# GAT layer and soft mixture of experts on one core: TensorE multiplies a step's share of the attention products before, not after, it turns the step's weights

## The chip, the core and the metric

The kernel runs on one core of one Trainium2 chip. A core has five engines with instruction streams of their own: TensorE (PE; its weight loads are listed as PEld), VectorE (DVE), ScalarE (ACT), GpSimd (POOL) and SyncE (SP), which here issues the transfers. They meet only through semaphores. The metric is the device time of one execution in microseconds (us). Before the change the median of three runs is 1707.67 us (1706.31 to 1708.2).

## The reference

1250 nodes with 768 features pass a two-layer graph attention network over 41250 edges (random edges both ways, and a loop at each node), and then a soft mixture of four experts; each adds to its input. The change lies in the first attention layer, with eight heads of 128 channels:

```
h = (x @ W1.T).reshape(n, 8, 128)
a_src = einsum('nhc,hc->nh', h, att_src);  a_dst = einsum('nhc,hc->nh', h, att_dst)
e = leaky_relu(a_src[src] + a_dst[dst], 0.2)
alpha = exp(e - segment_max(e, dst)[dst]);  alpha = alpha / segment_sum(alpha, dst)[dst]
out = segment_sum(alpha[:, :, None] * h[src], dst) + bias;  h1 = relu(out)
```

The second layer has one head of 768 channels. Everything is float32 at the interface.

## The kernel before

Edges are not followed one by one. The first stage builds a dense matrix `ln_c` with the logarithm of how often each source meets each destination (a large negative number where there is no edge), 1250 by 1250, in ten tiles of 128 destinations. With it, attention is dense: `attend_heads` (L911 to L1158) computes, for each head and each tile of destinations, a 128 by 1250 piece of logits, its softmax numerators, and their product with the head's features.

A **step** k is one head and one tile of destinations: head k // 10, tile j = k % 10, 80 steps in all. What each engine does for a step:

- POOL adds the row of the sources' part to the counts: `base` (L1006), two buffers deep.
- ACT computes relu of the scaled sum into PSUM, `at_r` (L1016), one buffer; it issues relu(k + 1) ahead of exp(k).
- DVE adds the two and takes the row maximum in one instruction, `logits(k)` (L1068), into a ring `q` of three; then negates the maximum (L1071).
- ACT takes the exponent of `q` in place (L1040), and reads the row sum off; that releases `at_p`.
- PE **turns** the step's weights: ten 128x128 transposes of `q` by the identity into `at_t` (L1134), three banks of PSUM, of which there is one set. Each bank is written once the step before has been read out of it.
- The turned weights are copied to `pt`: two banks by DVE (`read_turned(k - 1)`, L1077, after `logits(k)`), the third by ACT (L1044, after `exp(k)`). These copies release `at_read_low`, `at_read_mid` and `at_read_top`.
- PE multiplies: a head's output is made in three **chunks** of 4, 3 and 3 destination tiles, `DST_CHUNKS = ((0, 4), (4, 3), (7, 3))`. A chunk takes ten float32 products `at_o += h * pt` (L1155), one per tile of sources. They are dealt out to the steps by the table `PRODUCTS`; each entry is a chunk, how many heads back, the first source tile and how many:

```
    ((1, 1, 7, 3),), ((2, 1, 0, 3),), ((2, 1, 3, 4),), ((2, 1, 7, 3),),
    ((0, 0, 0, 3),), ((0, 0, 3, 2),), ((0, 0, 5, 3),), ((0, 0, 8, 2),), ((1, 0, 0, 3),), ((1, 0, 3, 4),),
```

So chunk 0 of a head is multiplied at j = 4 to 7, chunk 1 at j = 8, 9 and 0 of the next head, chunk 2 at j = 1, 2 and 3 of the next head. Ahead of a chunk's first product PE waits for two things: that all copies of the chunk's own destination tiles are made (for chunk 0 the last of them is step j = 3), and that the output bank, one of two, is free, which `at_h1_lo` tells.

A finished chunk is divided by the row sums, gets its bias and relu (DVE L1095 and L1097, three steps after its last product), is rounded to f16 by ACT (L1029), and the rest is stored by DVE (`low`, L1103), one step later; `low` releases `at_h1_lo`. Chunk 0 ends at j = 7, so its `low` is issued on DVE at j = 1, behind `read_turned` of the step before. The inverse row sums go through DRAM and back by transfers on SP (L982, L988), one chunk after the other. After step 79 no weights are left to turn; PE finishes the last products, and for the last chunk spreads the inverse sums itself (L1142). Every engine leaves the block before the second layer starts.

All orders here are written out by hand in the loops; no scheduler moves anything.

Of the kernel before, what the change touches and what calls it, by code (L numbers as in the profile page):

```python
# [32 lines left out]
P = 128  # L33
N = 1250
NT = -(-N // P)
# [17 lines left out]
BANK = 512  # L53
# [857 lines left out]
def attend_heads(nc, mem, sem, const, ln_c, h, h1, nad, s_row, in_s, bias_col, in_bias, a_rows, inv_rows):  # L911
# [8 lines left out]
    STEPS = HEADS * NT  # L920
    RING = 3
    base = mem("base", [P, 2, NP], F32)
    q = mem("q", [P, RING, NP], F32)
# [10 lines left out]
    neg_ready, p_ready, p_turned = sem("at_neg"), sem("at_p"), sem("at_pt")  # L934
    read_low, read_mid, read_top = sem("at_read_low"), sem("at_read_mid"), sem("at_read_top")
# [7 lines left out]
    def chunk_tiles(g):  # L943
        head, c = divmod(g, CHUNK)
        return head, DST_CHUNKS[c][0], DST_CHUNKS[c][1]


    def slices(k):
        head, j = divmod(k, NT)
        for c, back, first, units in PRODUCTS[j]:  # L950
            if 0 <= head - back < HEADS:
                yield (head - back) * CHUNK + c, first, units
# [9 lines left out]
    with (  # L962
# [6 lines left out]
        @block.sync  # L969
        def _(eng):  # L970
            def load_s(head):
                eng.wait_ge(in_s, 16 * head)
                eng.wait_ge(relu_ready, (head - 1) * NT)
                eng.wait_ge(base_ready, (head - 1) * NT)
                eng.dma_start(s_row[:, head % 2, :].rearrange("p (t n) -> p t n", t=NT),
                              a_rows[head * NT:(head + 1) * NT, :].unsqueeze(0).to_broadcast([P, NT, P]))\
                    .then_inc(in_s, 16)

            def turn_inverse(g):
                head, a, n = chunk_tiles(g)  # L980
                eng.wait_ge(factor_ready, g + 1)
                eng.dma_start(inv_rows[g, 0:n * P].rearrange("(t p) -> p t", p=P),  # L982
                              factor[:, head * NT + a:head * NT + a + n],
                              allow_slow_non_contiguous=True).then_inc(inv_kept, 16)
                eng.wait_ge(inv_kept, 16 * (g + 1))
                if g >= 2:
                    eng.wait_ge(divided, g - 1)
                eng.dma_start(inv[:, g % 2, 0:n * P],  # L988
                              inv_rows[g:g + 1, 0:n * P].to_broadcast([P, n * P])).then_inc(in_inv, 16)

            for head in range(HEADS):
                for c in range(CHUNK):
                    if head * CHUNK + c < LAST:
                        turn_inverse(head * CHUNK + c)
                    if c == CHUNK - 1 and head + 2 < HEADS:
                        load_s(head + 2)
# [128 lines left out]
        @block.tensor  # L1125
        def _(eng):
            for k in range(STEPS + NT):
                if k < STEPS:
                    eng.wait_ge(p_ready, k + 1)
                    for b, read in enumerate((read_low, read_mid, read_top)):  # L1130
                        if k >= 1:
                            eng.wait_ge(read, k)
                        for t in range(b * (BANK // P), min((b + 1) * (BANK // P), NT)):
                            mm = eng.transpose(tp[:, t * P:(t + 1) * P], q[:, k % RING, t * P:(t + 1) * P],  # L1134
                                               const["ident"][:, :])
                        mm.then_inc(p_turned, 1)
                if k == STEPS + 1:
                    n = chunk_tiles(LAST)[2]
                    eng.wait_ge(read_low, STEPS)
                    eng.wait_ge(spread_ready, n)  # L1140
                    for i in range(n):
                        mm = eng.matmul(tp[:, i * P:(i + 1) * P], const["ones"][:, :], spread[:, i * P:(i + 1) * P],  # L1142
                                        start=True, stop=True)
                    mm.then_inc(inv_turned, 1)
                for g, first, units in slices(k):
                    head, a, n = chunk_tiles(g)
                    if first == 0:

                        last = head * NT + a + n
                        for read in (read_low, read_mid, read_top):  # L1150
                            eng.wait_ge(read, last)
                        if g >= 2:
                            eng.wait_ge(h1_lo, g - 1)
                    for t in range(first, first + units):
                        mm = eng.matmul(op[:, g % 2, 0:n * P], h[:, head, t, :], pt[:, a:a + n, t, :],  # L1155
                                        start=t == 0, stop=t == NT - 1, skip_group_check=True)
                    if first + units == NT:
                        mm.then_inc(out_done, 1)  # L1158


def second_layer(nc, mem, sem, banks, const, ln_c, pn, pt, h1t, z, v2, x2t, xw, w2t, fw1, bias, x_in, a_rows, x_out, phi,
# [1084 lines left out]
```

## Time and profile before

| | |
|---|---|
| median of 3 runs | 1707.67 us |
| the profiled execution | 1710.9 us, its span 1709.1 us |
| steps of the first attention layer | from 316.9 us (first turn) to 619.6 us (last `low`) |
| in that stretch (316.9 to 620): PE, DVE, ACT, POOL busy | 278.2, 264.8, 244.6, 218.9 us of 303.1 |
| idle PE ahead of the turns, waiting for ACT's exponent | 35.9 us, 33 times, of which 16.5 before the first |
| granted TensorE clock in that stretch, mean | 0.96 |

The span is what the profiler saw of one execution; the profiled execution's own time is 1.8 us longer. Busy times overlap, because the engines work side by side. A clock of 1.00 is 2.4 GHz, 0.50 is 1.2 GHz. In rows of the timeline the columns are the start in us, how long the row's instructions took together, the engine, line and operation, output<-inputs, shapes and xcount; brackets at the end give the idle time before the row and what ended it. Instructions in a row are merged where they follow each other. The profiler lists two records for each float32 product of L1155 and one for each transpose, so x6 is three products, x8 four and x4 two.

### The profile page before, as it was taken

The page shows a single profiled execution, that of the slowest core. Times are in us where ns is not written, and L with a number is a line of the kernel's source. Part 1 is how long each engine was busy: PE and PEld are TensorE (multiplying, and loading weights), DVE is VectorE, ACT ScalarE, POOL GpSimd, SP SyncE. Part 2 cuts the span into 40 slices and gives each one's busy share as a digit, 9 for nine tenths or more (in the row PEclk, how much of TensorE's full clock was granted, in tenths as well). Part 3 has the DMA queues.
Part 4 walks back from the last instruction along what each step waited for, and adds up shares of the span by engine and source line. Part 5 has one row for each costly group of instructions (what it writes and reads, how often), then busy time and mean ns, then how long its engine had stood idle before and what let it go on. Part 6 is the DMA issues. An engine that isn't in the chain of part 4 may idle for free. (4 is left out here: it accounts for less than half of the span.)

```text
span 1709.1 us, 24928 instructions
## 1 busy us (share of the span) xinstructions
PE 1557.3 (91%) x8615; PEld 882.5 (52%) x8615; DVE 1102.0 (64%) x1810; ACT 846.2 (50%) x1322; POOL 272.4 (16%) x120
## 2 busy tenths in 40 slices
PE   6896666599999989999999899999999989999999
PEld 3442332366666545555554455555555545555555
DVE  7989999699999937553332456666666666766200
ACT  3159999688888827421111333333333335656000
POOL 1000000687877707000000000000000000000000
PEclk9998889699999989999999999999999998999999
DMA  4000100023232336441210544444444446783211
GB/s 180 19 29 27 44 19 11 4 34 37 32 50 34 22 81 164 103 134 56 56 47 28 133 116 117 116 117 117 119 119 119 119 124 206 214 214 98 74 56 53
DMA packets 204683, 146.91 MB, mean 86 GB/s; under 512 B 171758, under 2 KB 173768, under 8 KB 204464
## 3 DMA queue, kind: packets, MB, share of 16 engines
q1 hardware_dynamic: 204592, 145.75, 33.8%
q8 instruction: 51, 0.84, 0.3%
q14 instruction: 40, 0.33, 0.1%
HBM read 78.70 MB, written 28.35 MB: 63 GB/s over the span
## 5 line engine op out<-in xcount | busy, mean ns | idle before, releaser
L1006 POOL TENSOR_TENSOR base<-s_row,ln_c 128x1250 f32<-128x1250 f32 x80 | 227.6, 2847 | 58.5 <-DVE top L1068 56.2
L102 PE MATMUL sl_di<-x2t_hi,ph_hi 128*128 128x512 f16 (+1 forms) x576 | 195.5, 339 | 0.3 <-PEq L1226 0.3
L104 PE MATMUL sl_di<-x2t_hi,ph_lo 128*128 128x512 f16 (+1 forms) x576 | 195.5, 339 | 0.0
L103 PE MATMUL sl_di<-x2t_lo,ph_hi 128*128 128x512 f16 (+1 forms) x576 | 195.5, 339 | 0.0
L1155 PE MATMUL at_o<-pt,h 128*128 128x384 f32 (+1 forms) x480 | 188.2, 530 | 1.9 <-DVE h L1103 1.9
L901 PE MATMUL fs<-one_src,one_dst 128*128 128x512 f16 x720 | 120.4, 324 | 63.7 <-ACT one_dst L812 54.6
L1134 PE MATMUL at_t<-ident,q 128*128 128x128 f32 x800 | 108.1, 285 | 36.7 <-ACT q L1040 35.9
L1134 PEld LDWEIGHTS at_t<-ident,q 128*128 128x128 f32 x800 | 93.6, 146 | 79.7 <-ACT q L1040 69.7
L647 DVE TENSOR_SCALAR one_src<-iota,src,worth 128x625 f16<-128x625 f16 x360 | 131.9, 442 | 3.2 <-PE fs L901 2.1
L1016 ACT ACTIVATE at_r<-s_row,nad 128x1250 f32<-128x1250 f32 x80 | 104.5, 1307 | 37.8 <-DVE top L1068 37.1
L901 PEld LDWEIGHTS fs<-one_src,one_dst 128*128 128x128 f16 x720 | 56.8, 106 | 126.9 <-ACT one_dst L812 73.2
L1068 DVE CUSTOM_DVE_ANT_0 q<-at_r,base 128x1250 f32<-128x1250 f32 x80 | 116.2, 1453 | 5.5 <-POOL base L1006 3.6
L1077 DVE COPY pt<-at_t 128x512 f32<-128x512 f32 x160 | 103.2, 685 | 23.0 <-PE at_t L1134 22.6
L1155 PEld LDWEIGHTS at_o<-pt,h 128*128 128x128 f32 x480 | 86.8, 194 | 57.5 <-issue 27.6
L2076 PE MATMUL co_c<-hid_hi,ps_hi 128*128 128x385 f16 x320 | 105.9, 331 | 8.7 <-DVE ps_lo L2010 8.7
L102 PE MATMUL sl_di<-xw,pt_hi 128*128 (+1 forms) x320 | 105.3, 329 | 7.4 <-DMA pt_lo<-pn_lo 5.7
L1787 DVE TENSOR_REDUCE top<-lg 128x1 f32<-128x1250 f32 x32 | 46.5, 1454 | 98.4 <-ACT lg L1721 86.0
L1040 ACT ACTIVATE q<-q,neg_top 128x1250 f32<-128x1250 f32 x80 | 105.9, 1323 | 0.1
L2080 PE MATMUL co_c<-hid_hi,ps_lo 128*128 128x385 f16 x320 | 105.4, 329 | 0.0
L103 PE MATMUL sl_di<-xw,pt_hi 128*128 (+1 forms) x320 | 105.3, 329 | 0.0
L104 PE MATMUL sl_di<-xw,pt_lo 128*128 (+1 forms) x320 | 105.3, 329 | 0.0
L2078 PE MATMUL co_c<-hid_lo,ps_hi 128*128 128x384 f16 x320 | 105.0, 328 | 0.0
(270 smaller groups left out, 3137.9 us busy)
## 6 DMA issues: line engine op xcount, KB each, us to landing
logits_t<-lg SPq DMA_DIRECT2D x32, 625.0 KB, 3.2
phf<-in_phi SPq DMA_DIRECT2D x32, 384.0 KB, 3.5
logits_in<-logits_t SPq DMA_DIRECT2D x16, 640.0 KB, 5.5
logits_in<-logits_t SPq DMA_DIRECT2D x16, 610.0 KB, 5.3
w2f<-in_w2t SPq DMA_DIRECT2D x16, 384.0 KB, 3.4
s_row<-a_rows SPq DMA_DIRECT2D x9, 640.0 KB, 6.5
ew1f<-in_fw SPq DMA_DIRECT2D x6, 768.0 KB, 5.3
wf<-in_fw SPq DMA_DIRECT2D x12, 384.0 KB, 6.2
```

The costliest lines, as they stand in the source:

```text
L102: eng.matmul(out, lh, rh, start=first, stop=False, skip_group_check=True)
L103: eng.matmul(out, lh, rl, start=False, stop=False, skip_group_check=True)
L104: return eng.matmul(out, ll, rh, start=False, stop=last, skip_group_check=True)
L647: eng.tensor_scalar(one_src[:, place(b, i), 0:HALF], const["iota"][:, 0:HALF], src[:, ds(col, 1)], worth[:, ds(col, 1)], ALU.is_equal, ALU ...
L901: mm = eng.matmul(counts(g)[:, a:a + n], one_dst[:, place(b, i), :], one_src[:, place(b, i), a:a + n], start=False, stop=b == PIECES - 1 a ...
L1006: eng.tensor_tensor(base[:, k % 2, 0:N], s_row[:, head % 2, 0:N], ln_c[:, j, 0:N], ALU.add)\
L1040: eng.activation(q[:, k % RING, 0:N], q[:, k % RING, 0:N], ACT.Exp, bias=neg_top[:, k:k + 1], accum_out=den[:, k:k + 1]).then_inc(p_ready, 1)
L1068: eng.tensor_tensor_reduce(q[:, k % RING, 0:N], rp[:, 0:N], base[:, k % 2, 0:N], 1.0, -MASK / 2, ALU.add, ALU.max, top[:, k:k + 1]).then_i ...
L1134: mm = eng.transpose(tp[:, t * P:(t + 1) * P], q[:, k % RING, t * P:(t + 1) * P], const["ident"][:, :])
L1155: mm = eng.matmul(op[:, g % 2, 0:n * P], h[:, head, t, :], pt[:, a:a + n, t, :], start=t == 0, stop=t == NT - 1, skip_group_check=True)
L2076: eng.matmul(cp[:, bank, 0:HID + 1], high, hid[0][:, slot, 0:HID + 1], start=begin, stop=False, skip_group_check=True)
L2080: mm = eng.matmul(cp[:, bank, 0:HID + 1], low, hid[0][:, slot, 0:HID + 1], start=False, stop=end, skip_group_check=True)
```

## The change

In PE's loop over the steps the block that turns the step's weights moves from the head of the loop body to its end, behind the products dealt to that step. Waits, counts and tiles stay as they are; so do the programs of the other engines.

```
             for k in range(STEPS + NT):
-                if k < STEPS:
-                    eng.wait_ge(p_ready, k + 1)
-                    for b, read in enumerate((read_low, read_mid, read_top)):
-                        if k >= 1:
-                            eng.wait_ge(read, k)
-                        for t in range(b * (BANK // P), min((b + 1) * (BANK // P), NT)):
-                            mm = eng.transpose(tp[:, t * P:(t + 1) * P], q[:, k % RING, t * P:(t + 1) * P],
-                                               const["ident"][:, :])
-                        mm.then_inc(p_turned, 1)
                 if k == STEPS + 1:
...
                 for g, first, units in slices(k):
...
                     if first + units == NT:
                         mm.then_inc(out_done, 1)
+                if k < STEPS:
+                    eng.wait_ge(p_ready, k + 1)
+                    for b, read in enumerate((read_low, read_mid, read_top)):
...
+                        mm.then_inc(p_turned, 1)
```

PE's program around the first product of a chunk 0 (step j = 4 of the second head), before. `at_t` rows are transposes, `at_o` rows products, of 512 columns for chunk 0 and 384 for the others:

```order
L1155 MATMUL at_o<-pt_10595,h_95 128x384 x3
L1134 MATMUL at_t<-ident_49,q_10594 128x128 [waits at_read_low,at_p]
L1134 MATMUL at_t<-ident_49,q_10594 128x128 x3
L1134 MATMUL at_t<-ident_49,q_10594 128x128 [waits at_read_mid]
L1134 MATMUL at_t<-ident_49,q_10594 128x128 x3
L1134 MATMUL at_t<-ident_49,q_10594 128x128 [waits at_read_top]
L1134 MATMUL at_t<-ident_49,q_10594 128x128
L1155 MATMUL at_o<-pt_10595,h_95 128x512 [waits at_read_top,at_h1_lo,at_read_mid,at_read_low]
L1155 MATMUL at_o<-pt_10595,h_95 128x512 x2
```

Here the ten transposes are those of step j = 4, the products ahead of them those of j = 3. The same place now:

```order
L1146 MATMUL at_o<-pt_10595,h_95 128x384 x3
L1156 MATMUL at_t<-ident_49,q_10594 128x128 [waits at_read_low,at_p]
L1156 MATMUL at_t<-ident_49,q_10594 128x128 x3
L1156 MATMUL at_t<-ident_49,q_10594 128x128 [waits at_read_mid]
L1156 MATMUL at_t<-ident_49,q_10594 128x128 x3
L1156 MATMUL at_t<-ident_49,q_10594 128x128 [waits at_read_top]
L1156 MATMUL at_t<-ident_49,q_10594 128x128
L1146 MATMUL at_o<-pt_10595,h_95 128x512 [waits at_read_top,at_h1_lo,at_read_mid,at_read_low]
L1146 MATMUL at_o<-pt_10595,h_95 128x512 x2
L1156 MATMUL at_t<-ident_49,q_10594 128x128 [waits at_read_low,at_p]
```

The rows read alike, but the transposes ahead of the chunk's first product are now those of step j = 3, whose copies that product waits for; those of j = 4 stand behind it, in the last row. The step's products have moved ahead by one set of transposes.

PE's program from j = 0 to j = 1 of the second head, where chunk 2 of the first head starts, before (the first row is j = 0, the transposes are those of j = 1):

```order
L1155 MATMUL at_o<-pt_10595,h_95 128x384 x3
L1134 MATMUL at_t<-ident_49,q_10594 128x128 [waits at_read_low,at_p]
L1134 MATMUL at_t<-ident_49,q_10594 128x128 x3
L1134 MATMUL at_t<-ident_49,q_10594 128x128 [waits at_read_mid]
L1134 MATMUL at_t<-ident_49,q_10594 128x128 x3
L1134 MATMUL at_t<-ident_49,q_10594 128x128 [waits at_read_top]
L1134 MATMUL at_t<-ident_49,q_10594 128x128
L1155 MATMUL at_o<-pt_10595,h_95 128x384 [waits at_read_top,at_h1_lo,at_read_mid,at_read_low]
```

And now:

```order
L1146 MATMUL at_o<-pt_10595,h_95 128x384 x3
L1156 MATMUL at_t<-ident_49,q_10594 128x128 [waits at_read_low,at_p]
L1156 MATMUL at_t<-ident_49,q_10594 128x128 x3
L1156 MATMUL at_t<-ident_49,q_10594 128x128 [waits at_read_mid]
L1156 MATMUL at_t<-ident_49,q_10594 128x128 x3
L1156 MATMUL at_t<-ident_49,q_10594 128x128 [waits at_read_top]
L1156 MATMUL at_t<-ident_49,q_10594 128x128
L1146 MATMUL at_o<-pt_10595,h_95 128x384 [waits at_read_top,at_h1_lo,at_read_mid,at_read_low]
L1146 MATMUL at_o<-pt_10595,h_95 128x384 x2
L1156 MATMUL at_t<-ident_49,q_10594 128x128 [waits at_read_low,at_p]
```

Again the transposes between are a step earlier: those of j = 0 now, with those of j = 1 behind the product. DVE's `low` of j = 1, on which `at_h1_lo` counts, stands on DVE behind the copies of j = 0.

## Rows read from the trace of the kernel before

**Rows 1.** Windows of the attention steps: three heads' worth, then all of it.
```profile
core 0: us, PE busy (x) PEld busy (x) DVE busy (x) ACT busy (x) POOL busy (x), PEclk, DMA share, GB/s
402.00:438.00 36.00, 33.99 (x163) 21.69 (x162) 33.69 (x64) 31.46 (x48) 28.94 (x11) 1.00 0.31 38
...
316.90:620.00 303.10, 278.17 (x1286) 178.87 (x1286) 264.79 (x493) 244.56 (x365) 218.91 (x77) 0.96 0.27 31
```

**Rows 2.** Waits between 317 and 602 us: waiter, waited for, us in total, times, longest.
```profile
PE at_t L1134 <- ACT q L1040: 35.9, 33, 16.5
```

**Rows 3.** Timeline of PE, one head and the next's start (j = 4 to j = 4).
```profile
439.44 1.31 PE L1134 MATMUL at_t<-ident,q 128*128 128x128 f32 x10 [0.37 <-ACT q L1040]
440.58 2.74 PE L1155 MATMUL at_o<-pt,h 128*128 128x512 f32 x6
443.16 1.26 PE L1134 MATMUL at_t<-ident,q 128*128 128x128 f32 x10
444.25 1.88 PE L1155 MATMUL at_o<-pt,h 128*128 128x512 f32 x4
445.97 1.26 PE L1134 MATMUL at_t<-ident,q 128*128 128x128 f32 x10
...
450.39 1.31 PE L1134 MATMUL at_t<-ident,q 128*128 128x128 f32 x10 [0.59 <-ACT q L1040]
...
454.83 2.10 PE L1155 MATMUL at_o<-pt,h 128*128 128x384 f32 x6
456.77 1.25 PE L1134 MATMUL at_t<-ident,q 128*128 128x128 f32 x10
457.86 2.75 PE L1155 MATMUL at_o<-pt,h 128*128 128x384 f32 x8
460.44 1.25 PE L1134 MATMUL at_t<-ident,q 128*128 128x128 f32 x10
461.53 2.10 PE L1155 MATMUL at_o<-pt,h 128*128 128x384 f32 x6
...
471.42 1.26 PE L1134 MATMUL at_t<-ident,q 128*128 128x128 f32 x10
472.51 2.10 PE L1155 MATMUL at_o<-pt,h 128*128 128x384 f32 x6
474.98 1.31 PE L1134 MATMUL at_t<-ident,q 128*128 128x128 f32 x10 [0.37 <-ACT q L1040]
```

**Rows 4.** Timeline of all engines, DVE and ACT at j = 4.
```profile
470.72 1.45 DVE L1068 CUSTOM_DVE_ANT_0 q<-at_r,base 128x1250 f32<-128x1250 f32 x1
...
474.83 0.36 ACT L1044 ACTIVATE pt<-at_t 128x256 f32<-128x256 f32 x1
```

**Rows 5.** Timeline of all engines, DVE at j = 1.
```profile
462.82 0.68 DVE L1103 TENSOR_TENSOR h<-at_o,h 128x512 f16<-128x512 f32 x1
```

**Rows 6.** Timeline of all engines: a division on DVE, a first weight load.
```profile
445.00 0.56 DVE L1095 TENSOR_TENSOR at_o<-at_o,inv 128x384 f32<-128x384 f32 x1
...
445.60 0.63 DVE L1097 TENSOR_SCALAR at_o<-at_o,bias_act 128x384 f32<-128x384 f32 x1
...
456.58 1.20 PEld L1134 LDWEIGHTS at_t<-ident,q 128*128 128x128 f32 x10 [0.26 <-ACT q L1040]
```

**Rows 7.** Timeline of the steps' end, behind the transposes of step 79.
```profile
601.59 4.68 PE L1155 MATMUL at_o<-pt,h 128*128 128x384 f32 x14
...
608.82 8.38 PE L1155 MATMUL at_o<-pt,h 128*128 128x384 f32 x20 [1.89 <-DVE h L1103]
```

**Rows 8.** Window inside those last products (columns as in rows 1).
```profile
610.00:613.00 3.00, 3.00 (x6) 1.54 (x5) 0.97 (x2) 0.49 (x1) 0.00 (x0) 0.50 0.00 0
```

**Rows 9.** Timeline of the first head (its window 310 to 330 last).
```profile
319.45 2.40 PE L1134 MATMUL at_t<-ident,q 128*128 128x128 f32 x10 [0.15 <-ACT q L1040]
...
333.12 4.56 PE L1155 MATMUL at_o<-pt,h 128*128 128x512 f32 x6
...
310.00:330.00 20.00, 9.58 (x40) 7.98 (x40) 13.52 (x25) 14.59 (x19) 16.82 (x7) 0.50 0.00 1
```

More of the change, by code:

```diff
@@ L1158, in _ @@
                         mm.then_inc(out_done, 1)
+                if k < STEPS:
+                    eng.wait_ge(p_ready, k + 1)
+                    for b, read in enumerate((read_low, read_mid, read_top)):
+                        if k >= 1:
+                            eng.wait_ge(read, k)
+                        for t in range(b * (BANK // P), min((b + 1) * (BANK // P), NT)):
+                            mm = eng.transpose(tp[:, t * P:(t + 1) * P], q[:, k % RING, t * P:(t + 1) * P],
+                                               const["ident"][:, :])
+                        mm.then_inc(p_turned, 1)
 def second_layer(nc, mem, sem, banks, const, ln_c, pn, pt, h1t, z, v2, x2t, xw, w2t, fw1, bias, x_in, a_rows, x_out, phi,
```

## The prediction

> **What bounds the kernel now.** I read the windows first. In the attention steps PE is busy 33.99 of 36 us, DVE 33.69 and ACT 31.46 [rows 1]: three engines within 7% of each other, so neither "PE is the bound" nor "PE is free" is a reading; what counts is how they hand a step on. The waits come next. PE waits for ACT's exponent 33 times, 35.9 us in all, of which 16.5 is the start of the layer [rows 2]; 19.4 us are left, spread in pieces of under 1 us.
>
> Then PE's timeline, one head from the turn of j = 4 to the next head's: 439.44 to 474.98, 35.54 us [rows 3]. PE's own part I take from start to start where the second of two groups did not wait. Turn to products: 443.16 to 444.25, 1.09. Products to the next turn: three of chunk 0 440.58 to 443.16, 2.58; two of them 444.25 to 445.97, 1.72; three of the 384-column ones 454.83 to 456.77, 1.94; four of those 457.86 to 460.44, 2.58 [rows 3]. A step is thus 3.67, 2.81, 3.03 or 3.67, and a head by the table of products 2 x 3.67 + 2 x 2.81 + 4 x 3.03 + 2 x 3.67 = 32.42 us. The other 3.12 us of a head are the spread waits. The clock is 1.00 throughout [rows 1].
>
> **What the change removes: cover.** No instruction is added or dropped on any engine. PE's sequence T0 P0 T1 P1 T2 ... (T the turn, P the products of a step) becomes P0 T0 P1 T1 P2 T2. Seen from the turns, P(k) is now done between T(k - 1) and T(k): one step earlier. That is harmless where a chunk is under way. At a chunk's start it isn't, and three starts per head have three answers.
>
> *Chunk 0, at j = 4.* Its first product waits for the copies of T(3). Before, T(4) stood between, and T(4) waits for those copies anyway, bank by bank, so the wait was met. Now P(4) comes right behind T(3), and PE, which runs its program in order, keeps T(4) queued behind it. The last copy is ACT's third bank, which ACT issues behind exp(4), and exp(4) needs the logits that DVE started at 470.72. In the trace T(3) starts at 471.42 and leaves PE free at 472.51, where P(3) starts; the ACT copy ends at 474.83 + 0.36 = 475.19 [rows 3, 4]: a gap of 2.68. It gets longer, because T(3) itself moves ahead: between T(2) and T(3) now stand the three products of j = 3 (1.94) in place of the four of j = 2 (2.58), 0.64 earlier, while DVE and ACT don't move. With some 0.1 for the semaphore the stall is 3.4 us. In the first head nothing precedes (no 0.64) and a turn takes 2.40 instead of 1.26 [rows 9], so 3.4 - 0.64 - 1.14 = 1.6.
>
> *Chunk 2, at j = 1.* Its first product waits for `low` of chunk 0, which DVE issues at j = 1 behind the copies of T(0). Before, P(1) stood behind T(1), and was never late. Now it is behind T(0). PE would be free at 461.53; `low` ends at 462.82 + 0.68 = 463.50 [rows 3, 5]: 1.97, again 0.64 more (three products of j = 0 in place of four of j = 9), and 0.1 to 0.2: 2.8 us.
>
> *Chunk 1, at j = 8.* It needs T(6) copied and the `low` that DVE issued at j = 7. Both are over before T(7), which waits for exp(7), is done. Nothing.
>
> Stalls: 7 x 3.4 + 1.6 + 7 x 2.8 = 45.0 us (the eighth start of a chunk 2 lies behind step 79, where it waits as now).
>
> **What comes back.** The spread waits. They arise where the ring T(k), DVE's copies, logits(k + 2), exp(k + 2), T(k + 2) is slower than PE. Without anything else on DVE that ring took from 450.39 (T(7)) to the weight load at 456.58 (T(9)), 6.19 us [rows 3, 6]; two steps of PE's own are 5.8 to 6.5. After a stall PE is the late one and works back to back, so most of the 3.12 goes. What stays is the division inside the ring: 445.00 to about 446.1, 1.1 us more [rows 6]; one of the three divisions of a head (that at j = 6) falls where no stall covers it: 6.19 + 1.1 - 6.48 = 0.8, and a remainder of some 0.3 a step on. So 2.0 of 3.12 come back. Bounds: nothing, or all 3.12. Seven heads: -14.0 (0 to -21.8).
>
> The end: the four products of j = 9 now go ahead of the last turn, so PE's rest behind it is 2.58 shorter: -2.6 (bounds 0 and -2.6, since DVE's division of the last chunk but two could keep the end where it is). The transfers of the inverse sums get more time per head, not less; nothing is charged to them. Without the clock: 45.0 - 14.0 - 2.6 = 28.4 us.
>
> **The clock.** PE has no idle stretch above 0.8 us in the steady heads, and the clock stays at 1.00. At the end of the steps PE idled 1.89 us, and inside the 20 records of the last chunk, which followed it, the window 610 to 613 shows 0.50, that is 1.2 GHz, though PE was busy all 3 us [rows 7, 8]. Ten such products took 8.38 us; at full clock they are 10/3 x 1.94 + 0.16 = 6.6. A fall cost 1.8 us. Every stall of the new order but that of the first head (where the clock is at 0.50 in any case [rows 9]) is longer than those 1.89 us: 14 falls x 1.8 = 25.2. Bounds: none falls, 0; or each takes in a turn (2.40 for 1.26) and a share of chunk 0 (4.56 for 2.74) [rows 3, 9], 3.0 each, 41. Because PE is the late engine behind a stall, I count them in full.
>
> The Trainium skill, page "TensorE: Matmul & The Clock Gate", section "HAM oscillation — how this bites in real kernels", says that a kernel in which PE waits between short bursts of matmuls can fall back to the low clock at each wait, and pays at every one. By that rule the term stands as here. Read to the letter, though, it asks for a longer idle stretch than this trace's 1.89 us before a fall, and by that the shorter of the two stalls might be spared; the trace disagrees, but it shows one case only, so that reading is rival 2.
>
> **Sum.** 28.4 + 25.2 = 53.6 us. On the profiled execution: span 1709.1 to 1762.7, time 1710.9 to 1764.5. That execution was 3.2 above the median of the runs, so for the median: 1707.67 + 53.6 = 1761.3 us. Its own range: 1750 (the clock term at 1.0 per fall) to 1773 (2.6 per fall).
>
> **Rivals.**
> 1. *The stalls come, the clock holds.* For it: the stalls are interrupted by dense work of some 12 to 20 us, and in the heads before nothing fell. Against: the one idle stretch of that size did bring it down. 1707.67 + 28.4 = 1736.
> 2. *Only one kind of stall brings the clock down*, the longer. 28.4 + 7 x 1.8 = 41.0: 1748.7.
> 3. *Faster: PE fills its waits.* The products are put where PE now waits for exp: T(k - 1), then P(k) while ACT is busy, then T(k). If the two chunk starts found their copies done, what remains is the gain, up to 3.12 x 7 + 2.6 = 24.4: 1683. It decides where DVE and ACT finish a step's copies within PE's 1.09 us behind a turn. Against: ACT's copy is issued behind the next step's exponent, and ended 2.68 us after PE was free [rows 4].
> 4. *No change*: stalls of a third of the size, just paid for by the waits that go (2.3 + 0.9 against 3.1 a head). It would need DVE and ACT to run ahead of the turns by a step, which their order in the program does not let them.
>
> **Chances.** The forecast 0.72, rival 1 0.11, rival 2 0.10, rival 3 0.04, rival 4 0.03. A difference under 0.2% (3.4 us) can't be told from no change here. Faster 0.04, same 0.03, slower 0.93. The range reaches down to rival 1 with a little of the uncertainty of what comes back, and up to the dearer falls: 1734 to 1776.
>
> **What the changed profile would show.** A wait of the products' first weight load for ACT's third-bank copy (L1044), eight times, about 3.4 us each; a wait for DVE's `low`, seven more times, about 2.8; PE's waits for exp down from 19.4 to some 8 us; a head of about 40 us at full clock and 43 with falls; and 0.50 in windows right behind the stalls, 14 of them. The clock at 1.00 all through the heads makes it rival 1. Waits of under 1 us at the chunk starts would make the forecast wrong at its root; heads above 45 us would say that a ring through DVE that I left out is lengthened by the stalls too.

## The result and the profile after

| | before | after |
|---|---|---|
| median | 1707.65 us (4 runs) | 1761.03 us (4 runs, 1756.02 to 1762.37) |
| ratio | | 1.0312, 95% interval 1.03 to 1.0324 |
| profiled execution, its span | 1710.9, 1709.1 us | 1762.37, 1760.6 us |
| first turn to the next layer's first transfer | 316.9 to 621.18 | 317.11 to 673.99 |

The forecast was 1761.3 us. The two spans differ by 51.5 us. The steps of the first attention layer are 52.6 us longer, and all else is 1.1 us shorter. One of the seven executions of the control in experiment 3 took 3287.44 us for a reason that isn't known, and its ratio leaves that one out.

The waits of the changed kernel from 317 to 658 us (waiter, waited for, us in total, times, longest; L1146 are the products now, L1156 the turns):

```profile
DVE pt L1077 <- PE at_t L1156: 79.4, 42, 6.1
...
PE at_o L1146 <- ACT pt L1044: 25.9, 8, 3.4
PE at_t L1156 <- ACT q L1040: 24.0, 13, 16.5
...
PE at_o L1146 <- DVE h L1103: 18.2, 7, 2.6
```

Two rows are new: the products wait for ACT's third-bank copy eight times and for DVE's `low` seven times, 44.1 us. The waits of the turns for ACT's exponent, which were there before [rows 2], have shrunk from 35.9 us in 33 waits to 24.0 in 13. The start of the layer is 16.5 us of each; without it they went from 19.4 to 7.5.

A chunk 0's start at j = 4, from the timeline of all engines; it answers to [rows 4] and the end of [rows 3]:

```profile
415.28 1.25 PE L1156 MATMUL at_t<-ident,q 128*128 128x128 f32 x10
...
416.78 1.28 DVE L1077 COPY pt<-at_t 128x512 f32<-128x512 f32 x2
...
418.01 1.32 ACT L1040 ACTIVATE q<-q,neg_top 128x1250 f32<-128x1250 f32 x1
418.06 0.53 DVE L1103 TENSOR_TENSOR h<-at_o,h 128x384 f16<-128x384 f32 x1
...
419.33 0.36 ACT L1044 ACTIVATE pt<-at_t 128x256 f32<-128x256 f32 x1
...
419.98 2.05 PE L1146 MATMUL at_o<-pt,h 128*128 128x512 f32 x2 [3.45 <-ACT pt L1044]
```

PE's turn of step j = 3 ends at 416.53. DVE copies its two banks, but ACT first makes the exponent of step 4 and only then copies the third bank, 419.33 to 419.69. The products start 0.29 later, after 3.45 us without work. And a start at j = 1, which answers to [rows 5]:

```profile
401.01 1.25 PE L1156 MATMUL at_t<-ident,q 128*128 128x128 f32 x10
...
404.05 0.68 DVE L1103 TENSOR_TENSOR h<-at_o,h 128x512 f16<-128x512 f32 x1
...
404.87 1.87 PE L1146 MATMUL at_o<-pt,h 128*128 128x384 f32 x3 [2.60 <-DVE h L1103]
```

Behind a stall comes the clock. PE's own timeline, a chunk 0's start in the third, the sixth and the seventh head (x6 is three products):

```profile
419.98 5.46 PE L1146 MATMUL at_o<-pt,h 128*128 128x512 f32 x6 [3.45 <-ACT pt L1044]
425.23 1.51 PE L1156 MATMUL at_t<-ident,q 128*128 128x128 f32 x10
...
553.58 2.81 PE L1146 MATMUL at_o<-pt,h 128*128 128x512 f32 x6 [3.42 <-ACT pt L1044]
556.23 1.26 PE L1156 MATMUL at_t<-ident,q 128*128 128x128 f32 x10
...
593.56 4.23 PE L1146 MATMUL at_o<-pt,h 128*128 128x512 f32 x6 [3.42 <-ACT pt L1044]
```

Windows of the same (the granted clock is the third number from the end of each row): a stretch before the first of these stalls, that stall with its products, and the products of the second:

```profile
409.00:418.00 9.00, 7.53 (x42) 5.34 (x40) 7.87 (x15) 5.13 (x8) 4.11 (x3) 1.00 0.52 95
418.50:425.50 7.00, 5.52 (x8) 2.35 (x9) 1.61 (x4) 3.85 (x6) 3.97 (x2) 0.53 0.06 1
...
554.00:557.00 3.00, 3.00 (x14) 1.67 (x13) 0.13 (x1) 2.34 (x3) 2.57 (x1) 1.00 0.00 0
```

The same three products take 5.46 us at 0.50, 2.81 at 1.00, and 4.23 where the clock changed within them. The stalls before them are all 3.42 to 3.45 us long. Of the seven such stalls after the first head, five were followed by products of 5.46 us, one by 4.23 and one by 2.81.

### The profile page after: what moved, and what is told of

It is laid out like the page before. It is cut to its first block and busy times, and to the rows that moved or that the text cites. A ratio compares the mean times of both kernels' runs of the same rounds, so it can differ in the third digit from the quotient of the medians.

```text
span 1760.6 us, 24928 instructions
## 1 busy us (share of the span) xinstructions
PE 1574.2 (89%) x8615; PEld 892.0 (51%) x8615; DVE 1100.1 (62%) x1810; ACT 847.5 (48%) x1322; POOL 270.9 (15%) x120
## 5 line engine op out<-in xcount | busy, mean ns | idle before, releaser
L1146 PE MATMUL at_o<-pt,h 128*128 128x384 f32 (+1 forms) x480 | 211.1, 581 | 46.0 <-ACT pt L1044 25.9
L1146 PEld LDWEIGHTS at_o<-pt,h 128*128 128x128 f32 x480 | 93.4, 208 | 113.0 <-issue 85.1
L1156 PEld LDWEIGHTS at_t<-ident,q 128*128 128x128 f32 x800 | 97.4, 148 | 65.9 <-ACT q L1040 38.9
L1156 PE MATMUL at_t<-ident,q 128*128 128x128 f32 x800 | 107.8, 285 | 24.2 <-ACT q L1040 24.0
```

## The experiments

Ratios are to runs of the kernel before on the same chip. Experiments 1 to 5 start from the changed kernel (2 restores the old order at two steps of ten); the control in 3 and experiment 6 start from the kernel before.

**1. Keep the array busy in the stalls.** If the stall and the clock behind it are two prices, filling part of the stall with matmuls whose results nobody reads pays one of them back.

```
                     if first == 0:
+                        fillers = {0: 5, 1: 0, 2: 3}[g % CHUNK]
+                        if fillers and k < STEPS:
+                            eng.wait_ge(read_low, k)
+                        for _ in range(fillers if k < STEPS else 0):
+                            eng.matmul(tp[:, 0:2 * P], const["ident"][:, :],
+                                       h[:, head, 0:2, :].rearrange("p t n -> p (t n)"),
+                                       start=True, stop=True, skip_group_check=True)
                         last = head * NT + a + n
```

> The changed kernel, with matmuls that serve nothing put into PE's two kinds of stall (five at j = 4, three at j = 1, 256 columns each, into the first bank of at_t as soon as that bank has been copied). The first 1.2 to 1.5 us of a stall stay idle, the rest is filled. The products still wait for the same copies and the same low. Theory A (my prediction): the stalls themselves cost some 28 us and the clock that falls behind them 25 us; with the array kept busy the clock stays at 1.00 and only the stalls remain: 1736 to 1741 us. Rival B: the low clock behind a stall is hidden by DVE and ACT, which are late there anyway, and the whole 53 us is the waiting: 1757 to 1765 us, with the clock at 1.00. Rival C: the clock falls all the same: 1758 to 1768.

Measured: 1737.15 us, ratio 1.0184 (1.0167 to 1.0201), where the change has 1.0312. PE's timeline at a chunk 0's start, then a wait (315 to 680 us) and a window over the heads from 405 to 640:

```profile
406.78 1.25 PE L1162 MATMUL at_t<-ident,q 128*128 128x128 f32 x10
409.02 2.43 PE L1143 MATMUL at_t<-h,ident 128*128 128x256 f32 x10 [0.98 <-DVE pt L1077]
411.45 2.81 PE L1152 MATMUL at_o<-pt,h 128*128 128x512 f32 x6
414.11 1.25 PE L1162 MATMUL at_t<-ident,q 128*128 128x128 f32 x10
```
```profile
PE at_t L1143 <- DVE pt L1077: 16.1, 14, 1.3
```
```profile
405.00:640.00 235.00, 216.50 (x1022) 143.14 (x1021) 192.07 (x362) 176.32 (x265) 155.09 (x55) 1.00 0.17 31
```

The products start as long after the turn as in the change (411.45 - 406.78 = 4.67; 419.98 - 415.28 = 4.70), but take 2.81 us in place of 5.46. The clock is 1.00 from 405 to 640, and a head takes 40.0 us (turn of a j = 0 at 394.17, the next at 434.20) against 44.7 in the change and 35.5 before. Theory A holds: of the 3.1% some 1.8 are the stalls, 1.3 (22 us) the clock. B, that the low clock is hidden, falls, and so does C, that the clock drops all the same. The changed kernel itself agrees: from its sixth to its seventh chunk 0, where no clock fell, it takes 593.56 - 553.58 = 40.0 us. One reservation: in experiment 1 the clock rose earlier in the first head too, which is worth some 1.2 us (first turn to eleventh 37.95 against 39.19 us).

**2. The old order at j = 1 and j = 4 alone.** Does the products' wait cost, or what no longer stands between two turns?

```
             for k in range(STEPS + NT):
+                if k < STEPS and k % NT in (1, 4):
+                    (turn step k)
...
-                if k < STEPS:
+                if k < STEPS and k % NT not in (1, 4):
                     (turn step k)
```

> The changed kernel with the old order (turn, then products) at j = 1 and j = 4 alone, the steps at which a chunk starts late. Products then wait for nothing that is late. Theory A': what is lost is the work that stood between two turns; T(3) and T(4), and T(0) and T(1), now follow each other directly, the second of each pair finds its exponent not made, and PE idles as long in front of the turn as it did in front of the products: 1750 to 1765 us, waits of the products gone, waits of the turns for ACT's exponent up by some 40 us. Rival D: the cost is the products' wait as such, because it holds the next turn back behind 2.6 us of products; with the turn first it goes: 1705 to 1725 us.

Measured: 1755.36 us, ratio 1.0287 (1.027 to 1.0304). Its waits from 315 to 680 us, where L1134 are the turns at j = 1 and 4, and PE's timeline from j = 3 to 5:

```profile
PE at_t L1134 <- ACT q L1040: 45.3, 16, 3.3
```
```profile
413.68 1.25 PE L1165 MATMUL at_t<-ident,q 128*128 128x128 f32 x10
417.88 1.31 PE L1134 MATMUL at_t<-ident,q 128*128 128x128 f32 x10 [2.95 <-ACT q L1040]
419.03 4.46 PE L1155 MATMUL at_o<-pt,h 128*128 128x512 f32 x10
```

The products within the heads wait for nothing, and sixteen turns wait instead, 45.3 us, about as much as the fifteen waits of the change (44.1). D, that the products' wait as such costs, falls. What the change took away is the work between T(3) and T(4), and between T(0) and T(1). With nothing there, PE idles in front of whichever comes next. A chunk's start is the place where no product is ready to fill that gap; it is not slow by itself.

**3. Another cut into chunks, so that chunk 0 needs one step less.**

```
-DST_CHUNKS = ((0, 4), (4, 3), (7, 3))
+DST_CHUNKS = ((0, 3), (3, 3), (6, 4))
```

> The changed kernel with a head's destinations cut into chunks of 3, 3 and 4 tiles instead of 4, 3 and 3, so that chunk 0 needs only the copies of step j = 2 when it starts at j = 4. Theory A: the eight waits for ACT's copy (25.9 us) and the falls of the clock behind them (16 us) go; what PE idled there shows up in part as waits for the exponent, and the seven waits at j = 1 stay: 1735 to 1748 us. Rival E: the products' start is not what counts, PE's turns are late because products stand ahead of them in every step: the wait moves to j = 5 or 6, 1755 to 1765.

> The kernel before with chunks of 3, 3 and 4 tiles: what that cut costs by itself. It moves the ten 512-column products to j = 1, 2 and 3, where four of them stand in j = 2 (3.4 us instead of 2.6), so turns there come later: 1708 to 1716 us. If the cut alone gained (under 1704), the run of the changed kernel with this cut would prove nothing about the chunk's start.

Measured: with the change's order 1741.72 us, ratio 1.0208 (1.0191 to 1.0225); with the order of before, the control, 1712.75, ratio 1.0034 (1.0022 to 1.0046). So under the change's order the cut gains 1.0%, though by itself it costs 0.3%. The waits of the first from 315 to 680 us, and PE at j = 3 and 4:

```profile
PE at_o L1146 <- DVE h L1103: 28.1, 15, 2.2
```
```profile
406.20 1.26 PE L1156 MATMUL at_t<-ident,q 128*128 128x128 f32 x10
409.01 2.17 PE L1146 MATMUL at_o<-pt,h 128*128 128x384 f32 x6 [1.56 <-DVE h L1103]
```

The eight waits for ACT's copy are gone, as A said, and the time lies in A's range. But the start at j = 4 was not made free: it now waits 1.56 us for `low`, the second thing a chunk's start waits for, which was hidden behind the copy. DVE issues the `low` of the chunk before last at j = 4, behind the copies of T(3): in the change it ended at 418.59, 1.1 before the copy. Neither my prediction nor the expectation of this run named it. E falls: no wait of the old size moved to j = 5 or 6.

**4. Divide a step earlier.** This frees the output bank sooner at both starts.

```
-                if k - 3 in done_at:      (ACT: high; DVE: divide)
+                if k - 2 in done_at:
...
-                if k - 4 in done_at:      (DVE: low)
+                if k - 3 in done_at:
```

> The changed kernel with a finished chunk divided two steps after its last product instead of three (and high and low a step earlier too), so that low of chunk 0 is made at j = 0 and the output bank is free when chunk 2 starts at j = 1. Theory A: the seven waits for low (18.2 us) and their falls (9 us) go, the eight waits at j = 4 stay or shrink a little since DVE's division leaves j = 3: 1728 to 1742 us. Rival F: PE then only waits for the next exponent instead, because DVE sets the pace: 1752 to 1762.

Measured: 1730.16 us, ratio 1.0143 (1.0126 to 1.0159). Waits from 315 to 680 us:

```profile
PE at_t L1156 <- ACT q L1040: 35.3, 40, 16.5
...
PE at_o L1146 <- ACT pt L1044: 17.9, 8, 2.4
```

No wait for `low` is left within the heads. The eight at j = 4 are down from 3.4 to 2.4 us: DVE no longer divides at j = 3, ahead of the logits on which exp(4) and so the copy depend, and those logits start 1.04 us before the turn T(3) (407.13, 408.17) where they started 0.06 before it (415.22, 415.28). F, that the time would stay above 1752, falls.

**5. Both.** The change's order with the cut of 3 and the lag of 4:

> Products first, chunks of 3, 3 and 4 tiles and the division a step earlier: both late chunk starts are taken away, the order of the change stays. Theory A: the whole loss goes, and since the tail is 2.6 us shorter and the clock holds, the time is about that of the kernel before: 1704 to 1713 us. Rival E: a loss of the order by itself stays: 1725 or more.

Measured: 1707.18 us, ratio 1.0001 (0.9992 to 1.001). Waits from 315 to 680 us, and the heads from 402 to 600:

```profile
PE at_t L1156 <- ACT q L1040: 40.3, 34, 16.5
```
```profile
402.00:600.00 198.00, 181.04 (x875) 116.86 (x874) 181.88 (x338) 168.97 (x253) 150.72 (x53) 1.00 0.23 32
```

No product waits within the heads, the clock is 1.00, and the loss is gone with the order of the change in place. A head takes 36.2 us (422.66 to 458.85), 0.7 more than before, and the end is shorter. The 0.7 comes with the cut, not with the order: the control, in the old order, takes 36.26 a head (387.73 to 423.99). So what cost was the late chunk starts, and the order shows no cost apart from them. The kernel before with both of these edits wasn't run. If their two ratios multiply, 1.0034 from the control and 0.9974 from experiment 6, it would stand at 1.001, an estimate, beside the 1.0001 measured here.

**6. The kernel before with the earlier division.** The version to which the experiments pointed:

> The kernel before with the division, high and low a step earlier. If DVE's tail work at j = 6, 0 and 3 is what makes PE wait there for the exponent, moving it to j = 5, 9 and 2, which hold other amounts of PE work, changes those waits: walked through the steps it gives 3 to 6 us less: 1702 to 1705 us. Rival: the inverse sums, which arrive 14 to 17 us after they are computed, are then late, and the DVE waits for them: 1708 to 1715.

Measured: 1703.17 us (10 runs), ratio 0.9974 (0.9964 to 0.9983). That is 4.4 us less than the kernel before on the same chip (1707.55): small, but outside the interval. Its end, from PE's timeline:

```profile
600.59 4.68 PE L1155 MATMUL at_o<-pt,h 128*128 128x384 f32 x14
605.11 0.83 PE L1142 MATMUL at_t<-spread,ones 128*128 128x128 f32 x6
605.77 6.62 PE L1155 MATMUL at_o<-pt,h 128*128 128x384 f32 x20
```

The size came, for another reason than I gave. Steps 0 to 79 are only 1.3 us shorter (first turn to last 282.3 against 283.6 us); the rest is here. The last chunk no longer waits 1.89 us for `low` [rows 7], and it takes 6.62 us against 8.38, at full clock. That the clock held because the wait went isn't shown: the change's own trace has the wait and holds too (below). The last products end at 612.39 instead of 617.20. The rival, late inverse sums, came in part: DVE waits for them four times, 6.1 us in all, where it was three times and 2.4, and after one of these waits (1.78) a turn waits 2.22 us.

## Why the prediction was right

By its own steps:

- **Which starts stall.** Right: eight at j = 4, seven at j = 1, none at j = 8.
- **The first kind.** 3.4 us forecast, 3.42 to 3.45 measured (1.6 and 1.94 in the first head); in total 25.9 for a forecast of 25.4. Taking the gap from one row of before and adding the 0.64 us by which the turn moves ahead was enough. The agreement is a little flattered, because the trace counts a stall from the end of the turn and the forecast counted from 1.09 us after its start. Counted that way it is 4.67 - 1.09 = 3.58 us (4.67 from turn to products in five of these stalls). The 0.1 us for the semaphore was too little; it took 0.29.
- **The second kind.** 2.8 forecast, 2.60 measured; 18.2 for 19.6.
- **What comes back.** 2.0 us of a head's 3.12, thus 14.0; waits of turns went from 19.4 to 7.5, 11.9. The better test is the head at full clock, 3.4 + 2.8 - 2.0 = 4.2 us longer by the forecast's terms: experiment 1 has 40.0 against 35.5, 4.5. The 19.4 were not all "pieces of under 1 us": besides two in the first head (2.21 and 1.58) one was 1.88, in the last head (below). And two steps of PE's own reach 3.03 + 3.67 = 6.7, not 6.5; the sum used the 6.48 of j = 6 alone, so it isn't touched.
- **The end.** -2.6 forecast. From the start of the last turn to the next layer it is 16.4 us (657.58 to 673.99) for 20.7 before: -4.3. The step missed 1.7 us. The fall of the clock from which I had priced all others stayed away there: the last chunk took 6.69 us and not 8.38, with the same 1.89 of idle before it:

```profile
658.67 2.10 PE L1146 MATMUL at_o<-pt,h 128*128 128x384 f32 x6
660.61 0.83 PE L1133 MATMUL at_t<-spread,ones 128*128 128x128 f32 x6
663.32 6.69 PE L1146 MATMUL at_o<-pt,h 128*128 128x384 f32 x20 [1.89 <-DVE h L1103]
```

- **The clock.** 14 falls at 1.8, 25.2 us. From the start of a stalled chunk's products to the next turn and on to that step's products, against 2.58 or 1.94 and 1.09 at full clock, the 14 stalls took 14.9 (j = 4), 8.3 (j = 1) and 1.9 us (the turns) more: 25.1. The sum is right, its factors are not: 11 stalls were followed by a low clock, at 2.3 each. Behind the long stall shown above the low stretch lasted some 7 us (418.5 to 425.5) and began before the products did. So a head with two falls takes 44.5 to 44.7 us, where the prediction expected 43. Experiment 1 shows the total from the other side, some 22 us. The count of 14 rested on one fall, "the one idle stretch of that size", and the trace of before has a second such stretch, which the prediction missed. In the last head a turn waits 1.88 us, and behind it the clock is 1.00:

```profile
594.13 1.31 PE L1134 MATMUL at_t<-ident,q 128*128 128x128 f32 x10 [1.88 <-ACT q L1040]
...
594.00:597.00 3.00, 2.87 (x14) 1.72 (x14) 2.94 (x6) 2.64 (x4) 0.30 (x1) 1.00 0.42 66
```

The evidence then was one fall in two, and the sentence "PE has no idle stretch above 0.8 us in the steady heads" is wrong there. Rival 1 deserved more than 0.11 on that record.

So rival 1 (no falls, 1736) is out by the windows and by the sum, and rival 2 (only the longer kind, 1749) because five of the seven shorter stalls were followed by the low clock too. Rival 3 (faster) and rival 4 (no change) are out by the 44.1 us of waits. Experiment 1 showed that stalls and clock are two prices, experiment 5 that both hang on the late chunk starts and not on the order by itself. Experiment 2 sharpens the cause: "cover removed", as the prediction headed it, is the better description than "products that wait".

Measured less forecast, the terms are -0.9 us for the stalls, +2.1 for what comes back, -1.7 for the end and -0.1 for the clock. They cancel by luck, and the clock's 14 x 1.8 for 11 x 2.3 cancels within itself. The 0.3 us between 1761.3 and 1761.03 are not the method's precision; for the profiled execution it was 1764.5 against 1762.37. Its own range of 1750 to 1773 tells more of that.

The Trainium skill's page "TensorE: Matmul & The Clock Gate", section "HAM oscillation — how this bites in real kernels", has the rule that waits between bursts of matmuls bring the clock down again and again. Here it is borne out as a tendency: 11 of 14.

## What to carry to other kernels

In a pipeline of turn, copy, multiply, look at what stands between a producer's two instructions on the engine that feeds the others: work moved out from between them is not slower, but the round trip that it covered appears. For each start of an accumulation ask for every condition, not only the latest; when the latest is mended the next one shows, as `low` did behind the copy. On TensorE count a stall of a few us twice, once as it is and once for the clock that may fall behind it, with a count of falls that you leave open; and try such a stall filled with useless matmuls before redesigning, since that tells the two apart in one run.

## What the hardware did that I had not expected

- The same stall doesn't have the same consequence: 3.42 us of idle were followed by products of 5.46, 4.23 or 2.81 us, and 2.60 us of idle by 3.45 to 3.87 us in five heads and 2.17 in two. The 1.89 us before the last chunk were followed by a low clock before the change (8.38 us) and not after it (6.69).
- Shorter stalls don't rule it out: 2.38 us at j = 4 in experiment 4 were followed by slower products (4.11 to 5.46 us in place of 2.81) in four of seven heads, 2.20 us at j = 1 in experiment 3 (4.42 to 4.51 in place of 2.81) in five of seven, and the 1.56 us at j = 4 there in none of seven. The one turn that waited 2.22 us in experiment 6 was followed by none (it took 1.31 us, and the clock from 498 to 501 is 1.00). What decides between two stalls of one length is not shown.
- Even with the stalls cut to 0.98 and 1.3 us of idle, 14 of them, the clock stayed at 1.00.
